# Two tiles of four images become eight units of one image, with the last add of a sampled column on the TensorE

## The chip, the cores and the metric

The kernel runs on one core of a Trainium2 chip, in float32 throughout. The metric is device time in microseconds (us) of one launch. Five engines work side by side, each through its own list of instructions in order, and meet only at semaphores: TensorE (PE; matmuls and transposes, its weight loads are listed as PEld), VectorE (DVE), ScalarE (ACT), GpSimd (POOL), and SyncE (SP, which here only issues transfers).

## The reference

The input is x, 8 images of 32 x 32 pixels with 64 channels. Two layers are added to it one after the other:

```
x = x + L0(groupnorm(x))      # groups of 2 channels, mean and variance over one image
x = x + L1(groupnorm(x))

L0: g, g1 = relu(bn(dwconv3x3(h, wg))), relu(bn(dwconv3x3(h, wg1)))
    gy, gx = sobel(h); Dx = 1/(gy*gy/4 + 1); Dy = 1/(gx*gx/4 + 1)
    D, c0, E, cm_x, cp_x, cm_y, cp_y = ...   # per pixel, from g, g1, Dx, Dy
    for _ in range(5):
        h' = D*(c0*h0 - 2E*h + cm_x*roll(h,1,w) + cp_x*roll(h,-1,w)
                + cm_y*roll(h,1,c) + cp_y*roll(h,-1,c)) + D*0.4*fsrc
        h0, h = h, h'
    return relu(bn(h))

L1: offsets and mask = conv3x3(x, w_offset) + b      # 27 numbers per pixel
    for each of 9 taps: bilinear sample of x at (y + dy, x + dx): 4 corners, 4 weights, times mask
    out = sum over taps and channels of sample * filt
```

L1 needs the finished L0 output of the whole image, since a tap may sample anywhere in it. Images are independent of each other throughout.

## The kernel before

**Tiles.** A tile is 4 images: a partition is an image row (4 x 32 = 128), and the free dimension holds the 32 columns times 64 channels, 2048 numbers. There are two tiles.

**Dense stage of a tile (L0, and the offsets of L1).** Group sums, the squares, the scale; transposes of the normalized input (`turn`), row matmuls for the Sobel gradients (`rows`), the two depthwise convolutions as matmuls with the transposed input as the weights (`conv 0` to `conv 3`), the coefficients, and 5 steps of 4 chunks of 512 numbers (`pde 0` to `pde 19`). In a chunk VectorE makes five products of coefficients and shifted h (L576, L580, L586), TensorE adds them up in a bank of PSUM (L1037), and VectorE adds the rest (L597). A chunk's sums on TensorE run while VectorE makes the next chunk's products, since four chunks are open to it. Then the second norm, the offset convolution, and `sampling`, which turns offsets into table indices and corner weights.

**The table.** The second norm's output is written to a table in HBM (L351): an entry is 1 KB, a pixel with its right, lower and lower right neighbours. At the start the whole table is cleared by 8 transfers (L338), from SP's queue.

**Columns.** A column of a tile is 128 pixels with 9 taps: GpSimd issues 9 indirect transfers (L378), each of which fetches 128 entries. VectorE multiplies the 4 corners of 9 taps by their weights (L748, 2304 numbers; in some columns of tile 0 ScalarE takes three taps, L910), adds lower to upper corners (L755, 1152) and right to left (L761, 576, into `sums`). TensorE transposes the sums, five times 128 x 128 (L1056), ScalarE copies them out of PSUM (L921), and TensorE multiplies by the filter (L1064). Every fourth column VectorE adds a group to x (L730) and SP stores it (L356). There are four pixel buffers. 64 columns x 9 taps are 576 gathers.

**Order.** `SCHEDULE` is a list written by hand: tile 0's dense stage alone, then tile 1's dense stage with tile 0's 32 columns between its pieces, then tile 1's 32 columns alone, in loops. Each engine takes its part of every piece in this order.

## Time and profile before

| | |
|---|---|
| Median of 3 runs | 1076.55 us (1072.9 to 1078.05) |
| Profiled execution, its own time | 1075.92 us |
| its span | 1074.0 us |
| First gather starts, last gather starts | 251.65 us, 1058.04 us |
| PE, DVE, ACT, POOL busy | 57%, 63%, 20%, 59% |
| TensorE clock granted, mean | 0.727 of full |

The page divides the span into 40 slices of 26.85 us. The digits are tenths of busy time, and in the row PEclk tenths of the full clock, 2.4 GHz: a 5 there is the lower of the clock's two levels, 1.2 GHz. A float32 matmul is two instructions; a transpose is one. The duration printed for a matmul contains its way through the array, so the distance between starts is what a row of matmuls costs. "Issue" in front of a gather is time in which GpSimd waits for nothing that the profile shows.

### The profile page before, as it was taken

How to read it: one execution, taken by the hardware profiler on the slowest of the kernel's cores; microseconds unless marked ns; L12 is line 12 of the kernel's file. 1: busy time of each engine (PE TensorE's matmuls, PEld its weight loads, DVE VectorE, ACT ScalarE, POOL GpSimd, SP SyncE). 2: the span in 40 equal slices, each digit the busy share in tenths (PEclk: the TensorE clock that was granted, in tenths of full speed). 3: DMA queues.
4: the chain of work that ended last, by engine and by line, in shares of the span. 5: the costliest groups of instructions: out<-in, count | busy, mean ns of one | idle time of the engine just before them, and what ended most of it. 6: DMA issues, size and time to landing. Idle time of an engine off the chain costs nothing.

```text
span 1074.0 us, 7428 instructions
## 1 busy us (share of the span) xinstructions
PE 612.7 (57%) x2314; PEld 399.3 (37%) x2314; DVE 673.2 (63%) x685; ACT 214.5 (20%) x577; POOL 628.6 (59%) x588
## 2 busy tenths in 40 slices
PE   1987999468985678958843667523222322322233
PEld 1773434123775244434323433323222322322233
DVE  6799999843788676858887446543344334334433
ACT  2721000022523223133213411200000000000000
POOL 0000000004888777877787777777777777777773
PEclk9998999779987878987975686655555555555555
DMA  6431000054222233233222583333333333333331
GB/s 217 132 120 43 0 0 1 0 110 111 84 74 74 79 93 93 77 87 95 85 83 88 133 254 105 93 106 103 107 99 105 107 97 107 101 107 98 106 107 56
DMA packets 58144, 100.35 MB, mean 93 GB/s; under 512 B 10168, under 2 KB 39040, under 8 KB 57856
## 3 DMA queue, kind: packets, MB, share of 16 engines
q0 software_dynamic: 27648, 75.53, 23.8%
q1 hardware_dynamic: 30464, 24.42, 8.4%
q8 instruction: 17, 0.28, 0.1%
q14 instruction: 15, 0.12, 0.0%
HBM read 79.13 MB, written 20.78 MB: 93 GB/s over the span
## 4 chain that ended last, share of the span: by engine, by line
POOL 58%; issue 20%; DVE 12%; PE 5%; ACT 2%; DMA 2%; SPq 1%; POOLq 0%; DVEq 0%
POOL pixels L378 57%; PE acc L1037 3%; DVE rsum L434 2%; SPq L351 1%; DVE shared L586 1%; DVE shared L576 1%; DMA table<-scratch 1%; DVE h_pad L597 1%; DVE shared L556 1%; DVE shared L580 1%; PE acc L959 1%; DMA x<-x_in 0%; DVE scratch L430 0%; DVE scratch L415 0%; PE acc L1005 0%
## 5 line engine op out<-in xcount | busy, mean ns | idle before, releaser
L378 POOL DMA_INDIRECT pixels<-table,index_now x576 | 626.3, 1087 | 180.2 <-issue 172.4
L748 DVE TENSOR_TENSOR pixels<-pixels,side 128x2304 f32<-128x2304 f32 (+1 forms) x64 | 148.2, 2315 | 260.8 <-DMA pixels<-table,index_now 260.4
L1056 PE MATMUL side<-const,sums 128*128 128x128 f32 x320 | 74.1, 388 | 352.7 <-DVE sums L761 324.4
L1037 PE MATMUL acc<-shared,const 128*128 128x512 f32 x400 | 196.1, 635 | 22.7 <-DVE shared L576 22.7
L1056 PEld LDWEIGHTS side<-const,sums 128*128 128x128 f32 x320 | 53.3, 199 | 369.4 <-issue 239.3
L370 POOL COPY index_now<-index 128x72 uint32 x8 | 2.1, 260 | 250.0 <-DMA table<-scratch 250.0
L921 ACT ACTIVATE sampled_T<-side 128x384 f32<-128x384 f32 (+1 forms) x128 | 49.7, 433 | 403.3 <-PE side L1056 403.2
L1064 PEld LDWEIGHTS side<-filt,sampled_T 128*128 128x128 f32 x640 | 126.3, 296 | 0.0
L1064 PE MATMUL side<-filt,sampled_T 128*128 128x64 f32 x640 | 125.8, 373 | 0.0
L1037 PEld LDWEIGHTS acc<-shared,const 128*128 128x128 f32 x400 | 77.8, 202 | 128.0 <-issue 108.3
L755 DVE TENSOR_TENSOR pixels<-pixels 128x1152 f32<-128x1152 f32 x64 | 86.9, 1358 | 7.4 <-ACT pixels L910 5.4
L910 ACT ACTIVATE pixels<-pixels,corner_w 128x64 f32<-128x64 f32 x228 | 56.5, 334 | 135.6 <-DMA pixels<-table,index_now 135.6
L586 DVE TENSOR_TENSOR shared<-arrays,h_pad 128x1024 f32<-128x1024 f32 x40 | 48.8, 1220 | 7.4 <-PE acc L1037 7.3
L580 DVE TENSOR_TENSOR shared<-arrays,h_pad 128x1024 f32<-128x1024 f32 x40 | 48.7, 1219 | 5.5 <-PE acc L1037 5.5
L761 DVE TENSOR_TENSOR sums<-pixels 128x576 f32<-128x576 f32 x64 | 48.5, 758 | 4.9 <-PE side L1056 0.5
L959 PE MATMUL acc<-conv_w,shared 128*128 128x256 f32 x128 | 39.5, 391 | 4.5 <-DVE h_pad L509 4.5
L576 DVE TENSOR_TENSOR shared<-arrays,h_pad 128x512 f32<-128x512 f32 x40 | 27.5, 688 | 18.4 <-ACT h_pad L800 18.4
L935 PE MATMUL acc<-rsum,const 128*128 128x64 f32 x16 | 4.9, 403 | 54.8 <-DVE rsum L434 54.0
L597 DVE TENSOR_TENSOR h_pad<-acc,shared 128x512 f32<-128x512 f32 x40 | 27.4, 685 | 2.1 <-PE acc L1037 2.1
L556 DVE TENSOR_TENSOR shared<-arrays,h_pad 128x512 f32<-128x512 f32 x40 | 27.6, 690 | 0.9
L1035 PE MATMUL acc<-arrays,const 128*128 128x512 f32 x50 | 25.5, 593 | 0.0
L935 PEld LDWEIGHTS acc<-rsum,const 128*128 128x128 f32 x16 | 3.6, 281 | 57.2 <-DVE rsum L434 55.6
(158 smaller groups left out, 744.0 us busy)
## 6 DMA issues: line engine op xcount, KB each, us to landing
table<-corner_w SPq DMA_DIRECT2D x8, 1225.0 KB
pixels<-table,index_now POOLq DMA_INDIRECT x576, 2.8
table<-scratch SPq DMA_DIRECT2D x16, 528.0 KB, 10.4
x<-x_in SPq DMA_DIRECT2D x2, 1024.0 KB, 7.2
out_dram<-x SPq DMA_DIRECT2D x16, 128.0 KB, 1.9
const<-const_in SPq DMA_DIRECT2D x1, 641.0 KB, 6.0
xn_next<-bn_in SPq DMA_DIRECT2D x1, 384.0 KB, 7.1
off_w<-offw_in SPq DMA_DIRECT2D x1, 288.0 KB, 7.1
```

Source lines behind the costliest of these rows:

```text
L378: pool.indirect_dma_start(out=pixels[:, w % COLS, k, :], out_offset=None, in_=table, in_offset=bass.IndirectOffsetOnAxis(ap=index_now[:, o ...
L580: dve.tensor_tensor(two(wc(prod[:, prod_slot(n, 1), :]), wc(prod[:, prod_slot(n, 2), :])), two(coef(2), coef("mid")), two(moved(0, -1), mo ...
L586: dve.tensor_tensor(two(wc(prod[:, prod_slot(n, 3), :]), wc(prod[:, prod_slot(n, 4), :])), two(coef(3), coef(0)), two(moved(-1, 0), moved( ...
L748: dve.tensor_tensor(quads[:, 0:cells, :], quads[:, 0:cells, :], weights[:, 0:cells].unsqueeze(2).to_broadcast([P, cells, C]), ALU.mult)\
L755: dve.tensor_tensor(px[:, :, 0:2 * C], px[:, :, 0:2 * C], px[:, :, 2 * C:4 * C], ALU.add)\
L761: dve.tensor_tensor(sums[:, j % 2, 0:K2 * C].rearrange("p (k c) -> p k c", c=C), px[:, :, 0:C], px[:, :, C:2 * C], ALU.add).then_inc(s_sum ...
L910: ins = act.activation(cell, cell, ACT.Copy, scale=corner_w[:, 0, w, 4 * k + q:4 * k + q + 1])
L921: act.activation(sampled_T[:, j % 2, a * P:b * P], turned[:, r, 0:(b - a) * P], ACT.Copy)\
L959: ins = pe.matmul(dst, turned_pair(dh, pair), w3[:, 0:4 * C], start=dh == 0, stop=False)
L1037: pe.matmul(bank(t, "pde", i), eye, prod[:, prod_slot(n, j), :], start=j == 0, stop=j == PRODS - 1)\
L1056: ins = pe.transpose(turned[:, r, (i - a) * P:(i - a + 1) * P], sums[:, j % 2, i * P:(i + 1) * P], eye)
L1064: ins = pe.matmul(out[:, j * C:(j + 1) * C], sampled_T[:, j % 2, k * P:(k + 1) * P], filt[:, k, :], start=k == 0, stop=k == TAP_PAIRS - 1)
```

## The change

The kernel is written anew around a smaller unit. What it does:

- **Units.** A unit is one image: a partition is an image row of one of four sides (a side is 8 columns wide), and the free dimension holds 8 columns times 64 channels, 512 numbers. There are 8 units. What crosses from a side to its neighbour goes through TensorE, with permuting matrices (`prev`, `next`, `halo`), 20 matrices in the constants instead of 4.
- **Order.** `BESIDE` cuts the dense stage of a unit in 8 parts. Unit 0's runs alone; then part w of unit u+1 stands ahead of column w of unit u, on every engine. In the last unit the columns stand alone.
- **Steps.** A step is one piece of the whole unit. VectorE seeds the target bank in PSUM with c0 times h0 plus the forcing (two instructions of 512), then makes the products from the source bank (two of 1024, one of 512); TensorE adds them shifted into the target (9 matmuls). The next step's products need the finished target.
- **A column** is 128 pixels of one image, again 9 gathers. VectorE multiplies (L529) and adds lower to upper corners (L534); the add of right to left is gone. TensorE transposes left and right parts into the same place, 10 transposes that accumulate in pairs (`flip`), and filters the column before it (`filtered`). There are 7 pixel buffers.
- **Transfers.** Inputs come in 4 transfers for each unit, all queued ahead of the 8 that clear the table. Each unit writes its part of the table with 8 transfers (L304) and needs only its own part before its gathers start. Indices are read in place, no loop is left on any engine.

```diff
-MAKES = {"sum1": [("sum", 0, "dve")], ...
-SCHEDULE = [
-    (0, "sum1, centre1, square1, deviation1, scale1, turn, rows, sobel, denominator, conv 0, gates 0, conv 1, "
...
+BESIDE = ("sum1 centre1 square1 scale1 turn", "grad den conv-0 log seed", "dterms conv-1 da own coef",
+          "pde-0 pde-1", "pde-2 pde-3", "pde-4 final sum2 centre2", "square2 scale2 halo turn2", "off samp")
+ORDER = [(0, piece) for part in BESIDE for piece in part.split()]
+for u in range(UNITS):
+    for w in range(WS):
+        if u + 1 < UNITS:
+            ORDER += [(u + 1, piece) for piece in BESIDE[w].split()]
+        ORDER.append((u, f"column-{w}"))
...
+            load_x(0)
...
+            for u in range(1, UNITS):
+                load_x(u)
             sp.wait_ge(s_zeros, 1)
             for b in range(B):
                 sp.dma_start(table[b * TY * TX:(b + 1) * TY * TX, :] ...).then_inc(s_cleared, 16)
             sp.wait_ge(s_cleared, 16 * B)
...
+            for u in range(UNITS):
+                pool.wait_ge(s_table, 16 * TABLE_DMAS * (u + 1))
+                pool.wait_ge(s_index, u + 1)
+                for w in range(WS):
+                    col = u * WS + w
+                    if col >= NB:
+                        pool.wait_ge(s_weighted, col - NB + 1)
+                    for k in range(K2):
+                        pool.indirect_dma_start(out=pixels[:, col % NB, k, :], ...)
...
+            def step(u, m):          # VectorE
+                seq(dve.tensor_tensor(target(m), c0[:, :], source(m) if m == 0 else target(m), ALU.mult))
+                dve.tensor_tensor(target(m), target(m), force[:, :], ALU.add).then_inc(s_seeded, 1)
+                if m:
+                    dve.wait_ge(s_h, n)
+                for dirs in (slice(1, 5, 2), slice(2, 5, 2)):
+                    dve.tensor_tensor(prod[:, dirs, :], coef[:, dirs, :],
+                                      source(m).unsqueeze(1).to_broadcast([P, 2, WC]), ALU.mult).then_inc(s_prod, 1)
+                dve.tensor_tensor(prod[:, 0, :], coef[:, 0, :], source(m), ALU.mult).then_inc(s_prod, 1)
...
-                dve.tensor_tensor(sums[:, j % 2, 0:K2 * C].rearrange("p (k c) -> p k c", c=C),
-                                  px[:, :, 0:C], px[:, :, C:2 * C], ALU.add).then_inc(s_sums, 1)
+                upper, lower = weighted[:, col % 2, 0:2, 0:K2, :], weighted[:, col % 2, 2:4, 0:K2, :]
+                dve.tensor_tensor(upper, upper, lower, ALU.add).then_inc(s_added, 1)
...
+            def column(col):         # TensorE
+                pe.wait_ge(s_added, col + 1)
+                for r, (a, b) in enumerate(PARTS):
+                    for k in range(a, b):
+                        for q in range(2):
+                            ins = flip(turned[:, r, (k - a) * P:(k - a + 1) * P],
+                                       weighted[:, col % 2, q, 2 * k:2 * k + 2, :].rearrange("p k c -> p (k c)"),
+                                       eye, q == 0, q == 1)
+                    ins.then_inc(s_part, 1)
+                if col:
+                    filtered(col - 1)
```

How the order of instructions moves is shown at three places. First TensorE in the kernel before, at a column of tile 0 between the convolutions of tile 1: L959 to L964 are the convolutions, L1056 the transposes of a column, L1064 its filter.

```order
L959 MATMUL acc<-conv_w,shared 128x256
L961 MATMUL acc<-conv_w,shared 128x128
L964 MATMUL acc<-conv_w,shared 128x128
L1056 MATMUL side<-const,sums 128x128 x5
L1064 MATMUL side<-filt,sampled_T 128x64 x5
L959 MATMUL acc<-conv_w,shared 128x256
```

The same place in the changed kernel, column 1 of a unit between the two convolution banks of the next: `conv_w,xT` are the convolutions, `const,weighted` the transposes.

```order
L697 MATMUL banks<-conv_w,xT 128x128
L700 MATMUL banks<-const,weighted 128x128 x10
L697 MATMUL banks<-filt,sampled_T 128x64 x5
L697 MATMUL banks<-bn_shift,const 128x512
L697 MATMUL banks<-conv_w,xT 128x128
L697 MATMUL banks<-conv_w,xT 128x384 x2
```

A column's transposes are ten instead of five, and the second half of a unit's convolution stands behind them in TensorE's list.

VectorE in the kernel before, a column inside the steps of tile 1: L576 to L586 are products of a chunk, L597 its end, L748 to L761 the column, L556 the next chunk's start.

```order
L580 TENSOR_TENSOR shared<-arrays,h_pad 128x1024
L586 TENSOR_TENSOR shared<-arrays,h_pad 128x1024
L597 TENSOR_TENSOR h_pad<-acc,shared 128x8x64
L740 COPY side<-corner_w 128x144
L748 TENSOR_TENSOR pixels<-pixels,side 128x1536
L755 TENSOR_TENSOR pixels<-pixels 128x9x128
L761 TENSOR_TENSOR sums<-pixels 128x576
L556 TENSOR_TENSOR shared<-arrays,h_pad 128x512
```

VectorE in the changed kernel, the end of `pde-1`, column 3, and the start of `pde-2`: L455 and L456 seed, L463 and L465 are products, L529 and L534 the column.

```order
L463 TENSOR_TENSOR prod<-coef,banks 128x2x512 x2
L465 TENSOR_TENSOR prod<-coef,banks 128x512
L529 TENSOR_TENSOR weighted<-pixels,banks 128x9x4x64
L534 TENSOR_TENSOR weighted<-weighted 128x2x576
L455 TENSOR_TENSOR banks<-c,banks 128x512
L456 TENSOR_TENSOR banks<-banks,force 128x512
L463 TENSOR_TENSOR prod<-coef,banks 128x2x512 x2
```

A column is two instructions instead of three, and stands after every second whole step instead of between chunks.

SP in the changed kernel, from the last small input to the first table write: 28 transfers of units 1 to 7 stand ahead of the 8 that clear the table; before, one transfer (x of tile 1) stood there.

```order
L283 DMA filt<-filt_in 128x320
L265 DMA x_1<-x_in 32x512 x4
L265 DMA x_2<-x_in 32x512 x4
L265 DMA x_3<-x_in 32x512 x4
L265 DMA x_4<-x_in 32x512 x4
L265 DMA x_5<-x_in 32x512 x4
L265 DMA x_6<-x_in 32x512 x4
L265 DMA x_7<-x_in 32x512 x4
L289 DMA table<-corner_w 1225x1x256 x8
L304 DMA table<-xn 32x9x128 x2
L304 DMA table<-xn 32x8x128 x6
```

The clearing has moved behind 28 transfers, and the first table write behind it is a quarter of a tile's.

## Rows read from the trace of the kernel before

**Rows 1.** The page: span, busy time, slices of POOL and clock, chain.

```profile
span 1074.0 us, 7428 instructions
PE 612.7 (57%) x2314; PEld 399.3 (37%) x2314; DVE 673.2 (63%) x685; ACT 214.5 (20%) x577; POOL 628.6 (59%) x588
POOL 0000000004888777877787777777777777777773
PEclk9998999779987878987975686655555555555555
POOL 58%; issue 20%; DVE 12%; PE 5%; ACT 2%; DMA 2%; SPq 1%; POOLq 0%; DVEq 0%
```

**Rows 2.** Windows: PE, PEld, DVE, ACT, POOL busy, clock, DMA share, GB/s.

```profile
250.00:664.00 414.00, 293.37 (x1116) 180.86 (x1115) 297.16 (x312) 125.15 (x382) 327.54 (x278) 0.81 0.35 99
664.00:1058.00 394.00, 124.08 (x545) 110.18 (x543) 165.68 (x135) 31.32 (x84) 299.91 (x305) 0.52 0.35 103
```

**Rows 3.** Groups by form: busy us, mean ns | idle before, releasers.

```profile
L378 POOL DMA_INDIRECT pixels<-table,index_now x576 | 626.3, 1087 | 180.2 <-issue 172.4 <-POOL index_now L370 7.1 <-DVE sums L761 0.6
L748 DVE TENSOR_TENSOR pixels<-pixels,side 128x2304 f32<-128x2304 f32 x45 | 114.9, 2554 | 244.7 <-DMA pixels<-table,index_now 244.5
L755 DVE TENSOR_TENSOR pixels<-pixels 128x1152 f32<-128x1152 f32 x64 | 86.9, 1358 | 7.4 <-ACT pixels L910 5.4
L580 DVE TENSOR_TENSOR shared<-arrays,h_pad 128x1024 f32<-128x1024 f32 x40 | 48.7, 1219 | 5.5 <-PE acc L1037 5.5
L761 DVE TENSOR_TENSOR sums<-pixels 128x576 f32<-128x576 f32 x64 | 48.5, 758 | 4.9 <-PE side L1056 0.5
L597 DVE TENSOR_TENSOR h_pad<-acc,shared 128x512 f32<-128x512 f32 x40 | 27.4, 685 | 2.1 <-PE acc L1037 2.1
L861 ACT ACTIVATE arrays<-acc 128x512 f32<-128x512 f32 x16 | 9.0, 632 | 1.7 <-PE acc L1005 1.6
L873 ACT ACT_TABLE_LOAD x2 | 2.6, 1283 | 0.0
L640 DVE TENSOR_TENSOR arrays<-arrays 128x144 f32<-128x144 f32 x2 | 0.6, 308 | 0.1
```

**Rows 4.** Timeline of TensorE at full clock: start, duration, instruction.

```profile
9.21 0.69 PE L935 MATMUL acc<-rsum,const 128*128 128x64 f32 x2 [9.21 <-DVE rsum L434]
...
115.13 0.19 PEld L1037 LDWEIGHTS acc<-shared,const 128*128 128x128 f32 x1 [0.24 <-issue]
...
464.48 0.53 PEld L1056 LDWEIGHTS side<-const,sums 128*128 128x128 f32 x5 [1.86 <-DVE sums L761]
...
464.98 1.20 PEld L1064 LDWEIGHTS side<-filt,sampled_T 128*128 128x128 f32 x10
```

**Rows 5.** Timeline near the end, clock at its lower level.

```profile
1042.38 0.93 PEld L1056 LDWEIGHTS side<-const,sums 128*128 128x128 f32 x5 [8.37 <-DVE sums L761]
...
1058.04 0.94 POOL L378 DMA_INDIRECT pixels<-table,index_now  x1 [0.30 <-issue]
```

**Rows 6.** Windows around an idle stretch of TensorE (columns as rows 2).

```profile
340.00:345.00 5.00, 0.55 (x4) 0.36 (x3) 4.74 (x4) 3.38 (x6) 4.05 (x4) 0.50 0.36 105
345.00:350.00 5.00, 5.00 (x18) 3.97 (x19) 4.93 (x4) 0.00 (x0) 4.43 (x2) 0.50 0.17 52
350.00:355.00 5.00, 5.00 (x11) 2.15 (x10) 4.93 (x3) 0.00 (x0) 4.39 (x3) 0.84 0.18 52
```

**Rows 7.** Table transfers by line: ns min/median/max, first and last start.

```profile
L351 SPq DMA_DIRECT2D table<-scratch x16: 302/2692/3941, 224.5 to 624.8; - x16
L338 SPq DMA_DIRECT2D table<-corner_w x8: 957/10293/11264, 4.9 to 68.2; - x8
```

**Rows 8.** Window in which the clearing ends (columns as rows 2).

```profile
90.00:95.00 5.00, 5.00 (x13) 2.23 (x12) 4.96 (x3) 0.00 (x0) 0.00 (x0) 1.00 0.05 16
```

**Rows 9.** Timeline: a VectorE instruction with two SBUF inputs, and a gather.

```profile
319.38 2.29 DVE L492 SCALAR_TENSOR_TENSOR arrays<-arrays 128x2048 f32<-128x2048 f32 x1
...
320.46 2.02 POOL L378 DMA_INDIRECT pixels<-table,index_now  x1 [0.30 <-issue]
```

More of the change, by code:

```diff
@@ L23 @@
 STEPS = 5
+NDIR = 5
 LO = 2
@@ L57 @@
-C_ENT = C_BASE + W * 2 * K2
-C_ALL = C_ENT + TILES
-MAKES = {"sum1": [("sum", 0, "dve")], "square1": [("sum", 1, "dve")], "sum2": [("sum", 2, "dve")],
-         "square2": [("sum", 3, "dve")], "turn": [("turn", q, "act") for q in range(NBANK)],
-         "rows": [("rows", q, "act") for q in range(2 * NBANK)],
-         "own sums": [("own", q, "dve") for q in range(NBANK)],
-         "turn2": [("turn2", q, "act") for q in range(NBANK)]}
-MAKES.update({f"conv {i}": [("conv", q, "dve") for q in (2 * i, 2 * i + 1)] for i in range(4)})
@@ L118 @@
-COLUMN = ("weigh column", "turn column", "copy column")
-ORDER = [(0 if "column" in part or part.startswith("scale ") else tile, part)
-         for tile, pieces in SCHEDULE for piece in pieces.split(", ")
-         for part in (COLUMN if piece == "column" else (piece,))]
-PLAN = [(t,) + made for t, piece in ORDER for made in MAKES.get(piece, [])]
-AT = {made[:3]: n for n, made in enumerate(PLAN)}
+PARTS = ((0, 4), (4, TAP_PAIRS))
+NB = 7
+TABLE_DMAS = 2 * SIDES
+NAMES = ("ones", "eye", "prev", "next", "diff", "diff2", "smooth", "smooth_neg",
+         "diff_in_left", "diff_at_left", "diff_in_right", "diff_at_right",
+         "smooth_neg_in_left", "smooth_neg_at_left", "smooth_in_right", "smooth_at_right",
+         "minus", "prev_neg", "next_neg", "halo")
@@ L194, in build_program @@
[L194 to L203 removed]
+        x1 = [sb(f"x1_{u}", [P, WC]) for u in range(UNITS)]
@@ L780, in _ @@
+            for u, part in ORDER:
+                name, _, i = part.partition("-")
+                piece(u, name, int(i or 0))
+            add_group(UNITS * GROUPS_U - 1)
         @block.scalar
@@ new lines, in norm_root, with turned_main @@
+            def norm_root(u, which):
+                act.wait_ge(*emptied(u, f"square{which}"))
+                act.activation(grstd[:, :], gvar[:, :], ACT.Sqrt, bias=gn_eps).then_inc(s_sd, 1)
+            def turned_main(u, what):
+                act.wait_ge(s_full, full(u, what, 0))
+                for dh in (1, 0, 2):
+                    ins = act.activation(*shifted_rows(rows(xT[:, dh, 0:PAIRS * P]), rows(bank(u, what, 0)), dh),
+                                         ACT.Copy)
+                ins.then_inc(s_act, 1)
@@ L927, in _ @@
+            act.wait_ge(s_setup, 1)
+            prepare(ACT.Sqrt)
+            for u, part in ORDER:
+                name, _, i = part.partition("-")
+                piece(u, name, int(i or 0))
         @block.tensor
         def _(pe):
-            def group_sums(t, k):
-                pe.wait_ge(s_rsum, 2 * norm_index(t, k // 2 + 1) + k % 2 + 1)
-                if t == 0 and k == 0:
-                    pe.wait_ge(s_const, 16)
-                wait_bank_empty(pe, t, "sum", k)
-                pe.matmul(bank(t, "sum", k)[:, 0:C], ones_block, rsum[:, :], start=True, stop=True).then_inc(s_bank, 1)
@@ L1049, in turn_part, with wait_bank_empty @@
[L1049 to L1060 removed]
+            def wait_bank_empty(u, what, q=0):
+                n = AT[u, what, q]
+                before = [f for f in PLAN[:n] if f[3] == PLAN[n][3]]
+                if before and before[-1][4]:
+                    pe.wait_ge(*emptied(*before[-1][:3]))
```

1378 lines of the change are left out of this document (617 added, 761 removed).

## The prediction

> **What bounds the kernel now.** I read the page first: its slices show GpSimd empty for the first nine, then at 7 to 8 tenths to the end, and its chain puts 58% on GpSimd and 20% on "issue", which is the time between gathers [rows 1]. So the kernel is 251.65 us of work ahead of the first gather, then 576 gathers in a row, then a tail. The windows give the pace: 305 gathers in the last 394 us, 1.29 us each, 11.6 us for a column of 9 [rows 2]. The last gather starts at 1058.04, so the tail behind it is 1074.0 - 1058.04 = 16.0 us [rows 1, 5]. While the first tile's gathers ran beside the second's dense stage they came at 1.49 us each (414 / 278) [rows 2]. VectorE is 63% busy and TensorE 57%, and neither sets the end [rows 1]: the dense work of tile 1 is hidden behind tile 0's gathers, because big instructions of a four-image tile keep several banks open, and a wait of one finds work in another.
>
> The profiled execution took 1075.92 us, 1.9 more than its span and within 0.1% of the median; the sums below are made against it.
>
> **What the change does to this.** The gathers stay 576, of the same shape. What is bought is the head: the first gather needs one image, not four. What is paid is that seven dense stages, each of one image, now stand in the same in-order lists as the columns, and that within a unit nearly every piece waits for the one before. So the question is the period S of a unit: what is longer, 8 columns of gathers (93 us), or the chain of a dense stage with 8 columns in it.
>
> **Prices.** TensorE at full clock: weight loads of a row of 512-column matmuls start 0.19 + 0.24 = 0.43 us apart, so a float32 matmul (two instructions) of 512 columns costs 0.86, of 448 0.75, of 384 0.64, and of 128 or fewer 0.22, since ten weight loads take 1.20 and five transposes 0.53 [rows 4]. Behind the last one the result takes about 0.45 more: two 64-column instructions take 0.69 in all [rows 4]. VectorE: 512 numbers 0.69, 1024 1.22, and a column 2.55 + 1.36 = 3.9 without the add of 0.76 that goes; small ones 0.2 to 0.3 [rows 3]. ScalarE: 0.63 for 512, a table load 1.28 [rows 3]. TensorE's share of a column is 10 transposes and 10 filter instructions, 1.1 + 1.2 = 2.3.
>
> **The period, part by part**, at full clock, each from VectorE's end of one column to its end of the next. TensorE starts each part with the 2.3 of the column just ended.
> - Part 0: 2.3, group sum 0.9 + 0.45, reduce and centre 1.0, square 0.6, sum 1.35, reduce, root, reciprocal and three small ones 1.8, scale 0.7, six transposes 1.1, copies 0.9, weights 0.3, column 3.9 = 15.4.
> - Part 1: 2.3, gradients 5.6 (two of 448 and four of 64 make 2.4, one of 512, two of 448 and four of 64 make 3.2), then conv-0 with 0.86 + 3 x (0.22 + 0.64 + 0.64 + 0.22) = 6.0. ScalarE's logarithm stands in its list behind conv-0's relu, so it comes at 2.3 + 5.6 + 6.0 + 0.4 + 0.6 = 14.9, takes 0.7, the exponential 1.28 + 0.6, then five VectorE instructions 3.6, column 3.9 = 25.2. TensorE is idle for 11 us of it: the other half of the convolution stands behind this column's transposes.
> - Part 2: 2.3, conv-1 6.0, latency and relu 1.1, then TensorE's own sums 4.1 + 0.4 beside VectorE's gate and coefficient work, the last coefficient 0.7, column 3.9 = 18.6.
> - Parts 3 and 4, two steps each: seeds 1.4 and first product 1.2, TensorE's nine matmuls 1.9 + 2.1 + 0.9 = 4.9 + 0.4, products 3.0, column 3.9 = 14.9 each, 0.3 more for one copy of weights. TensorE's second step (1.2 + 4.9) ends as the column does, so nothing is gained by the column in its shadow.
> - Part 5: one step 7.9, the shift and add 2.8, sum, mean and centre 2.4, column 3.9 = 17.0.
> - Part 6: 2.3, sum 1.4, root chain 1.7, scale 0.7, transposes 1.3, copies 0.9, column 3.9 = 12.2.
> - Part 7: 2.3, offsets (19 matmuls, all small) 4.3 + 0.4, sampling 8 instructions to the index 2.5, 7 more 2.2, column 3.9 = 15.7.
>
> The sum is 134.2 us. It is longer than the 93 us of gathers, so GpSimd will wait for indices, which come only in part 7, and S is this chain.
>
> **The clock.** TensorE has 75 us of work in these 134, with idle stretches of 4 to 11 us. In the trace of before such a stretch costs the clock: TensorE was idle from 340 to 345, granted 0.50, and was busy all of 345 to 350 at 0.50 still; the higher level came back in the next window (0.84) [rows 6]. That is some 6.6 us of work at half speed, and at half speed five transposes take 0.93 instead of 0.53 [rows 4, 5]. Parts 1 and 2 begin behind such a stretch: 3.3 us lost each. Part 3 loses 2.5, part 0 runs at the low level whole (column +1.8, two sums and transposes +2.9: 4.7), part 6 loses 3.9, part 7 4.5. Together 22 us, so S = 156.
>
> The Trainium skill says in "TensorE: Matmul & The Clock Gate", "What's actually happening", that the throttled clock is the default and activity releases it. By that rule the low level in parts with gaps is what to expect, and rows 6 agree (0.50 behind the idle stretch); with the clock always released the sum would be that of the rival below.
>
> **The sum.** Clearing the table bounds the first gather. It was issued from 4.9 on and its transfers were nearly over in the window from 90 to 95 (DMA share 0.05), some 87 us [rows 7, 8]. Now 28 loads at about 0.4 us of issue and some small ones stand ahead: from 17.5 to 105. Unit 0's dense stage alone is the chain without columns, 134 - 8 x (3.9 + 2.3) = 85 us, so it is hidden by the clearing. The table write adds its issue (8 transfers of about 280 pieces against 1056 for 2.7 us: 0.7 each) and 5 to land: first gather at 116. Its bounds: 90 (the dense stage alone) and 130.
> - First column of unit 0: 9 gathers and landing 13, column 4: to 133.
> - Parts 1 to 7 of unit 1: 156 - 20 = 136: to 269.
> - Six more units: 6 x 156 = 936: to 1205.
> - Unit 7 has no unit beside it. Its index came 6 us before: 71 distances of 1.29 = 91.5, and the tail 16.0 (0.76 less on VectorE, 0.9 more for the transposes): 1205 - 6 + 0.5 + 91.5 + 16 = 1307, and with the 1.9 outside the span **1309 us**, 22% slower.
>
> A microsecond of S counts seven times. S would have to be 122 us to reach 1076.
>
> **Unknown prices.** Transposes that accumulate do not occur in the trace: between nothing more than now (0.107 each) and as a full matmul of 128 columns (0.22), which gives 1.1 for a column and 8 x 7 x 1.1 = 60 us in all; I take the lower, as the same instruction. Reads of shifted or broadcast operands on TensorE: no change against up to 10% of 60 us a unit, 40 us in all, I take none. Hand-overs between engines are in the prices above where rows have them; some 60 in a period at 0 to 0.1 us more are 0 to 6 us of S. Gathers may be faster or slower beside this VectorE work; GpSimd has 60 us of slack in a period, so this is nothing.
>
> **Rivals.**
> - The clock stays high. TensorE is at work in every part, and the window 250 to 664 had a mean of 0.81 with 71% busy [rows 2]. Then S = 134 and the time is 1309 - 7 x 22 = 1155. Against it: the idle stretches above are as long as that in rows 6. The chance is 0.17.
> - More waits than I see, or the dear end of the transposes: S of 170 and more, 1405 and up. 0.15.
> - Gathers set the pace (the other sign). If the dense chain hid in the gathers as tile 1's does now, S would be 8 x 11.6 plus, between units, what the index comes late: column 6 3.9, TensorE's part and offsets 7.0, sampling 2.5, start 0.5 = 14 and landing 2.8, less the 11.6 of column 7's gathers: 5. S = 98, and the time 1309 - 7 x 58 = 903. For it: VectorE's own work is only some 90 us a unit. Against it: in-order lists, and three hand-overs in each step. It decides where S falls below 122, 12 us under my sum at full clock. 0.05.
> - The change as a trade of VectorE for TensorE: a column saves 0.76 on VectorE and pays 0.5 to 0.9 on TensorE in the same chain; alone it would be worth under 0.3 us a column, 15 us in all, and decides nothing.
>
> In that third rival the pace of gathers would matter. A gather beside a VectorE instruction with both inputs in SBUF took 2.02 us, against 0.94 alone, ending with it [rows 5, 9]. The Trainium skill, "SBUF — State Buffer", "SBUF: two separate sides", has such an instruction hold the port that GpSimd shares. Now most have one operand in PSUM; by that rule the pace is nearer 1.25 than 1.49, and the sum stays as it is.
>
> **How the numbers follow.** Forecast: S about 156, own range 1210 to 1400, chance 0.63. Clock high 0.17 (1155, down to 1110), more waits 0.15, faster or no change 0.05. The 8-in-10 range is 1140 to 1410. Within 0.5% is about what runs of this kernel can't tell from none. Faster by more 0.04, within 0.01, slower 0.95.
>
> **What would show it.** First gather near 116; gathers in eight bursts of some 95 us with idle stretches of some 60 between, ended by VectorE's index; 156 us from unit to unit; part 1 the longest with TensorE idle in it; a granted clock near 0.75; VectorE and TensorE both under 65% busy and waiting for each other in the steps. I am wrong if gathers are even to the end, if the first starts after 130, or if a part takes 5 us less than its sum.

## The result and the profile after

The changed kernel takes 1275.89 us (median of 4 runs, 1272.1 to 1277.78); the kernel before took 1076.88 in the same runs. The ratio is 1.185, 95% interval 1.181 to 1.189: slower by 18.5%. The forecast was 1309. The profiled execution took 1272.1 us, 2.2 more than its span. Runs over 1.5% above the fastest of their kernel are in a slower state and enter no comparison; below, that holds for two runs of one kernel. First the page: span, busy time, slices of TensorE, GpSimd and the granted clock, and the chain by engine and by line (31.7 us a slice).

```profile
span 1269.9 us, 9355 instructions
PE 801.5 (63%) x3472; PEld 598.6 (47%) x3472; DVE 616.9 (49%) x836; ACT 205.5 (16%) x403; POOL 564.8 (44%) x589
PE   6764578546875668656585558855677565865434
POOL 1002774067710776027740477107760177503773
PEclk9885789557896679857787678965798568875555
PE 44%; DVE 30%; SPq 7%; issue 7%; POOL 6%; DMA 3%; ACT 3%; POOLq 0%; DVEq 0%
```

Before, GpSimd's row had nine empty slices and then none [rows 1]; now it has eight bursts with a gap behind seven of them, and the chain that was 58% GpSimd is 74% TensorE and VectorE. The 195.9 us between the two spans add up so: the first gather comes 135.1 earlier (116.58 against 251.65); the gathers themselves take 64.7 less (561.6 against 626.3, [rows 3]); GpSimd idles 403 us between gathers beyond the usual 0.30, against 8.5 before; the end behind the last gather is 1.0 longer. The groups, as in [rows 3] (busy, mean ns of one | idle before, releasers):

```profile
L343 POOL DMA_INDIRECT pixels<-table,index x576 | 561.6, 975 | 688.5 <-issue 575.4 <-DMA table<-xn 112.9 <-DVE weighted L529 0.3
L529 DVE TENSOR_TENSOR weighted<-pixels,banks 128x2304 f32<-128x2304 f32 x64 | 163.2, 2550 | 70.0 <-DMA pixels<-table,index 54.2 <-issue 14.9
L700 PE MATMUL banks<-const,weighted 128*128 128x128 f32 x640 | 137.4, 392 | 342.4 <-DVE weighted L534 342.4
L463 DVE TENSOR_TENSOR prod<-coef,banks 128x1024 f32<-128x1024 f32 x80 | 93.9, 1215 | 61.4 <-PE banks L697 61.4
L534 DVE TENSOR_TENSOR weighted<-weighted 128x1152 f32<-128x1152 f32 x64 | 86.9, 1358 | 2.2
```

TensorE stood idle for 342 us in front of the transposes of columns, waiting for VectorE's L534. One period of the middle, cut where VectorE ends a column: parts 0 to 7 of a unit (length; busy PE, PEld, DVE, ACT, POOL; clock, DMA share, GB/s).

```profile
715.76:733.76 18.00, 8.49 (x42) 7.61 (x42) 8.26 (x16) 4.75 (x9) 13.74 (x15) 0.59 0.36 106
733.76:760.36 26.60, 15.65 (x73) 11.43 (x73) 8.25 (x10) 7.19 (x11) 20.20 (x22) 0.82 0.34 102
760.36:780.46 20.10, 15.18 (x67) 11.14 (x68) 9.61 (x15) 3.78 (x9) 15.23 (x17) 0.84 0.38 111
780.46:798.56 18.10, 16.38 (x58) 10.51 (x59) 12.37 (x13) 0.77 (x2) 13.84 (x15) 0.79 0.38 109
798.56:813.53 14.97, 12.73 (x58) 7.66 (x58) 12.62 (x14) 0.77 (x2) 2.47 (x3) 1.00 0.09 27
813.53:830.10 16.57, 9.85 (x49) 6.22 (x49) 10.36 (x12) 1.40 (x3) 0.00 (x0) 0.97 0.00 0
830.10:845.76 15.66, 8.21 (x37) 7.52 (x38) 6.89 (x13) 4.35 (x9) 0.00 (x0) 0.50 0.36 72
845.76:866.95 21.19, 12.77 (x80) 12.67 (x80) 7.80 (x17) 3.25 (x7) 7.53 (x8) 0.67 0.17 46
```

No engine is full in any of them; nearest are TensorE in part 3 (90%) and TensorE and VectorE in part 4 (85 and 84%). GpSimd is done with a unit in part 4 and stands idle until part 7 gives it the next index. Now inside part 1, the longest, in the timeline (start, duration, instruction, idle before):

```profile
733.89 2.40 PE L700 MATMUL banks<-const,weighted 128*128 128x128 f32 x10 [5.17 <-DVE weighted L534]
737.55 5.82 PE L697 MATMUL banks<-xn,const 128*128 128x448 f32 x26
744.11 5.37 PE L697 MATMUL banks<-conv_w,xT 128*128 128x128 f32 x24
749.52 0.60 ACT L657 ACTIVATE gates<-banks 128x512 f32<-128x512 f32 x1 [5.54 <-PE banks L697]
750.01 0.71 ACT L661 ACTIVATE log_t<-t_arr,scalars 128x512 f32<-128x512 f32 x1
750.74 1.28 ACT L663 ACT_TABLE_LOAD   x1
752.67 0.69 DVE L417 SCALAR_TENSOR_TENSOR t_arr<-t_arr,banks 128x512 f32<-128x512 f32 x1 [7.97 <-ACT banks L663]
756.31 2.55 DVE L529 TENSOR_TENSOR weighted<-pixels,banks 128x2304 f32<-128x2304 f32 x1
760.31 1.97 PE L700 MATMUL banks<-const,weighted 128*128 128x128 f32 x8 [10.82 <-DVE weighted L534]
```

Gradients, the first half of the convolution, relu, logarithm, table load, VectorE's five, the column: one behind the other, with TensorE idle for 10.8 us at the end of it.

### The profile page after: what moved, and what is told of

Same layout as the page of the kernel before. It is cut to its first block, busy times and chain, and to the rows that moved or that the text cites. A ratio compares the mean times of both kernels' runs of the same rounds, so it can differ in the third digit from the quotient of the medians.

```text
span 1269.9 us, 9355 instructions
## 1 busy us (share of the span) xinstructions
PE 801.5 (63%) x3472; PEld 598.6 (47%) x3472; DVE 616.9 (49%) x836; ACT 205.5 (16%) x403; POOL 564.8 (44%) x589
## 4 chain that ended last, share of the span: by engine, by line
PE 44%; DVE 30%; SPq 7%; issue 7%; POOL 6%; DMA 3%; ACT 3%; POOLq 0%; DVEq 0%
PE banks L697 35%; DVE weighted L529 11%; PE banks L700 9%; POOL pixels L343 6%; DVE weighted L534 6%; SPq L289 5%; DVE prod L463 3%; DMA table<-corner_w 2%; SPq L265 1%; DVE banks L456 1%; DVE xn L378 1%; ACT L663 1%; DVE banks L455 1%; ACT gates L657 1%; DVE prod L465 1%
## 5 line engine op out<-in xcount | busy, mean ns | idle before, releaser
L343 POOL DMA_INDIRECT pixels<-table,index x576 | 561.6, 975 | 688.5 <-issue 575.4
L700 PE MATMUL banks<-const,weighted 128*128 128x128 f32 x640 | 137.4, 392 | 342.4 <-DVE weighted L534 342.4
L700 PEld LDWEIGHTS banks<-const,weighted 128*128 128x128 f32 x640 | 114.1, 205 | 365.4 <-DVE weighted L534 350.6
L697 PE MATMUL banks<-prod,const 128*128 128x448 f32 (+2 forms) x720 | 219.2, 457 | 31.4 <-DVE prod L463 31.4
L529 DVE TENSOR_TENSOR weighted<-pixels,banks 128x2304 f32<-128x2304 f32 x64 | 163.2, 2550 | 70.0 <-DMA pixels<-table,index 54.2
L697 PEld LDWEIGHTS banks<-prod,const 128*128 128x128 f32 x720 | 114.8, 201 | 120.2 <-issue 120.2
L697 PEld LDWEIGHTS banks<-filt,sampled_T 128*128 128x128 f32 x640 | 124.7, 293 | 0.0
L463 DVE TENSOR_TENSOR prod<-coef,banks 128x1024 f32<-128x1024 f32 x80 | 93.9, 1215 | 61.4 <-PE banks L697 61.4
L697 PE MATMUL banks<-filt,sampled_T 128*128 128x64 f32 x640 | 123.0, 368 | 0.0
L697 PE MATMUL banks<-conv_w,xT 128*128 128x384 f32 (+1 forms) x384 | 89.5, 391 | 0.0
L534 DVE TENSOR_TENSOR weighted<-weighted 128x1152 f32<-128x1152 f32 x64 | 86.9, 1358 | 2.2
```

The lines of the kernel that those rows point to most:

```text
L343: pool.indirect_dma_start(out=pixels[:, col % NB, k, :], out_offset=None, in_=table, in_offset=bass.IndirectOffsetOnAxis(ap=index[:, at:at ...
L463: dve.tensor_tensor(prod[:, dirs, :], coef[:, dirs, :], source(m).unsqueeze(1).to_broadcast([P, 2, WC]), ALU.mult).then_inc(s_prod, 1)
L529: dve.tensor_tensor(weighted[:, col % 2, :, 0:K2, :].rearrange("p q k c -> p k q c"), pixels[:, col % NB, :, :].rearrange("p k (q c) -> p ...
L534: dve.tensor_tensor(upper, upper, lower, ALU.add).then_inc(s_added, 1)
L697: return pe.matmul(dst, lhsT, rhs, start=start, stop=stop, skip_group_check=True)
L700: return pe.matmul(dst, data, moved, start=start, stop=stop, is_transpose=True, skip_group_check=True)
```

## The experiments

The theory: the chain of one unit's dense stage with eight whole columns in it sets the period (150.2 us from index to index in the middle six units), and the low clock of TensorE behind its idle stretches is part of it. The rivals: gathers set it; or the trade of a VectorE add for transposes matters more than the forecast said.

**Conv-1 ahead of column 1.**

```diff
-"grad den conv-0 log seed", "dterms conv-1 da own coef"
+"grad den conv-0 log seed conv-1", "dterms da own coef"
```

> The second half of a unit's convolution (conv-1) stands right behind the first in every list, ahead of column 1 instead of behind it; nothing else moves. Chain theory: TensorE works in the stretch of 10.8 us in which it now waits for column 1, and part 2 (20 to 22.5 us now) loses the 6.0 us of the convolution; its remaining sums (4.1 us at full clock, 8.2 at the lower) still start after column 1's transposes, so part 2 becomes 14 to 17 us. The period falls from 150.2 to about 145, the time from 1276 to about 1235 (1225 to 1245). Rival, that the period is set by the amount of work on VectorE or by gathers: the same work in another order, so no change (1270 to 1282).

Measured: 1221.99 us (1220.08 to 1222.77), ratio 1.136 to before (1.134 to 1.138); period 143.4. It is 54 us less than the changed kernel: part 2 fell from 20.9 (mean) to 14.4, and one piece moved ahead of one column, in the lists of TensorE and ScalarE, did it; the other parts moved by -1.5 to +2.1 and nearly cancel. The theory held, with a little more gained than its range (1225 to 1245) allowed.

**Columns where VectorE waits, inside the parts.** `|` marks the column.

```diff
+"sum1 centre1 | square1 scale1 turn", "grad den conv-0 | log seed", "dterms conv-1 | da own coef",
+"pde-0 | pde-1", "pde-2 | pde-3", "pde-4 | final sum2 centre2", "| square2 scale2 halo turn2", "off | samp"
```

> The same instructions, but each column stands inside its part, where VectorE waits for another engine, and not behind it: behind centre1, behind conv-0, behind conv-1, between two steps, behind the single step, ahead of square2, behind off. Chain theory: a column's 3.9 us on VectorE lies in a wait: 2.4 us less in part 0, 3.9 in part 1, some 9 in part 2 (the column, and conv-1 which now starts behind conv-0), 1.4 in parts 3 and 4 each (two steps are 13 us in any case), 3.9 in part 5, 2.5 in part 6, 3.9 in part 7, together about 28. Period 122, time about 1080 (1060 to 1130). Rival, amount of work: no change. Rival, that gathers set it: no change either, since they are the same.

Measured: 1179.89 us (1179.3 to 1180.24), ratio 1.097 (1.095 to 1.099); period 136.5, not 122. Missed by 100 us. The timeline shows one reason: column 0 now stands ahead of its pixels, whose gathers begin only behind the index.

```profile
659.34 0.20 DVE L501 TENSOR_SCALAR index<-above 128x72 uint32<-128x72 f32 x1
...
662.93 0.63 ACT L646 ACTIVATE squares<-xc 128x512 f32<-128x512 f32 x1 [1.47 <-DVE xc L370]
673.02 2.56 DVE L534 TENSOR_TENSOR weighted<-pixels,banks 128x2304 f32<-128x2304 f32 x1 [9.90 <-issue]
...
677.02 2.39 PE L705 MATMUL banks<-const,weighted 128*128 128x128 f32 x10 [15.37 <-DVE weighted L539]
679.21 1.74 PE L702 MATMUL banks<-filt,sampled_T 128*128 128x64 f32 x10
680.79 1.11 PE L702 MATMUL banks<-squares,const 128*128 128x128 f32 x8
```

And the marker moved TensorE's part of a column together with VectorE's: the sum of squares, ready at 663.6, stands behind both at 680.8. A column has to be cut into its parts, each placed for its own engine.

**The third add back on VectorE.**

```diff
+                dve.tensor_tensor(left, left, right, ALU.add).then_inc(s_added, 1)
...
-                        for q in range(2): ins = flip(..., weighted[:, col % 2, q, ...], eye, q == 0, q == 1)
+                        ins = flip(..., weighted[:, col % 2, 0, ...], eye)
```

> The part of the change that its name speaks of, undone alone: VectorE adds right to left corners as well (576 numbers, 0.76 us), TensorE transposes 5 times in a column instead of 10. Chain theory: 0.76 us more in each of the 8 columns of a period and 0.5 (full clock) to 1.1 us (lower clock) less on TensorE in the same chain: between -0.3 and +0.3 us a column, so 1276 within 10 us either way. Rival, that accumulating transposes are dear: faster by 30 us or more. Rival, that VectorE's amount of work sets the pace: 7 x 8 x 0.76 = 43 us slower.

Measured: 1317.73 us (1315.37 to 1320.59), ratio 1.225 (1.222 to 1.228); period 157.2, clock 0.71. So that part of the change, alone, is worth 42 us, nearly three times the 15 that the prediction had as its bound. The rival "amount of work on VectorE" had 43 and met the number, but not as a mechanism: VectorE is 49% busy in the changed kernel, and with the same work in the woven order below a period is 47 us shorter. Two more runs below go into it.

**TensorE kept busy** with useless matmuls while it waits for a column.

```diff
+FILL = (16, 40, 12, 0, 0, 16, 16, 30)
+                if 0 < col < (UNITS - 1) * WS:
+                    pe.wait_ge(s_sT, (col - 1) * len(PARTS) + 1)
+                    for i in range(FILL[col % WS]): mm(turned[:, 0, 0:P], eye, M["ones"], True, True)
```

> TensorE gets matmuls whose result nobody uses (16, 40, 12, 0, 0, 16, 16, 30 of 128 columns ahead of columns 0 to 7), in the stretches in which it waits for a column's add, into a place that the transposes behind them overwrite. They should end before the add does at full clock. Clock theory: the granted clock rises from 0.74 to over 0.9, the period falls by 10 to 14 of the 16 us by which it exceeds the 134 of full clock: 1165 to 1205 us. Rival, that the lower clock lies where nothing waits for TensorE: clock up, time unchanged or a little more, since the extra matmuls can only be in the way (1270 to 1300).

Measured: 1174.24 us (1173.8 to 1175.8), ratio 1.0925 (1.090 to 1.095); clock 0.884, period 136.5. The time was inside the forecast, the clock stayed just under the 0.9 forecast. Adding work took 102 us off: the low clock is 13.7 us of a period at least. Three parts of it, 0, 3 and 6 (columns as above):

```profile
797.05:812.62 15.57, 11.13 (x73) 10.75 (x74) 8.30 (x15) 4.75 (x9) 11.91 (x13) 0.78 0.37 108
722.55:737.19 14.64, 12.75 (x56) 7.67 (x56) 12.33 (x14) 0.77 (x2) 11.29 (x12) 1.00 0.36 107
768.73:781.48 12.75, 10.06 (x64) 9.87 (x65) 7.13 (x14) 4.34 (x9) 0.00 (x0) 0.73 0.42 84
```

They last 18.0, 18.1 and 15.7 in the changed kernel at 0.59, 0.79 and 0.50. The forecast's sums at full clock were 15.4, 14.9 and 12.2. Part 2 gained nothing: it took 21.5 at 0.84 with the fillers and 20.9 at 0.80 to 0.84 without, against a sum of 18.6 at full clock.

**The third add at a high clock**: the last two edits together.

> The third VectorE add back (five plain transposes a column), with the useless matmuls that held the clock at 0.884 and 1174 us. Without them the third add cost 42 us (1318 against 1276) at a lower clock (0.71 against 0.743). Theory A 'the trade is near even, the 42 us came by the clock': at a high clock +0.76 on VectorE and -0.53 on TensorE, 0.23 x 56 = 13 us, 1187. Theory B 'VectorE's add stands in the chain whole, TensorE's transposes of the column before mostly don't': +0.76 x 56 = 43 us, 1217.

Measured: 1229.76 us at a clock of 0.847 and 1248.14 at 0.839, ratio 1.152 (1.142 to 1.162). The other two runs took 1255.01 (the profiled one, 0.825) and 1257.87 (0.829) and are not compared. The size is rough, then: 56 to 74 us over the run with fillers alone. Both theories missed, on the same side. What is firm is parts that ran at clock 1.00 with the add and without it. Part 1, this run (25.2 in each of its six middle units, 25.0 with the fillers alone), and part 4, from the run with the third add and no fillers (14.97 in the changed kernel):

```profile
723.59:748.81 25.22, 22.54 (x147) 18.33 (x147) 8.82 (x10) 7.19 (x11) 19.13 (x21) 1.00 0.36 105
```

```profile
833.60:849.38 15.78, 12.20 (x51) 7.12 (x51) 13.40 (x15) 0.77 (x2) 0.02 (x1) 1.00 0.03 9
```

Where TensorE's column leads the part, the trade costs 0.2, as the forecast had it. In the steps VectorE's seeds cover TensorE's transposes, so the five that are saved give nothing back and the add counts whole, 0.8. As an estimate from these two parts, with three columns in the steps and five elsewhere, that makes 3 x 0.8 + 5 x 0.2 = 3.4 us a period, 24 in all. The rest of the 42 I put down to the clock (0.743 to 0.71); this pair of runs doesn't show it alone, but the later run with this edit in another order does for its own case.

**A third of the gathers.** Only taps 0 to 2 are fetched (`for k in range(3)`, `pixels[:, :, 3:K2, :]` zeroed once).

> Only taps 0 to 2 of each column are fetched (192 gathers instead of 576), the other six are zeros written once at the start; VectorE and TensorE do all they did. Leaves out the samples of six taps. Theory 'the chain of dense stage and columns sets the period': the index period stays at 148 to 152 us, since nothing in it waits for a gather but column 0 after the index (54.2 us of waits for pixels in all, x7, 7.7 each). Of these 7.7 some 7.5 go (6 gathers less), so the period falls to about 143; the last unit's columns, 11.5 apart now, come at VectorE's and TensorE's own pace of 6 to 7 (-36 us), and the first column comes 7.5 earlier. Sum 1276 - 7 x 7.5 - 36 - 7.5 = 1180, 1160 to 1230. Theory 'gathers set the pace': a column costs 9 x 1.25 = 11.3 in every unit, and 3.8 with a third of them: 64 x 7.5 = 480 us less, about 800.

Measured: 1210.37 us (1198.96 to 1213.15), ratio 1.1235 (1.117 to 1.131); the last six periods have a mean of 150.4. With 384 gathers less the period did not move: gathers don't set it, and the rival is out. The time lies in the expected range (1160 to 1230), but the period of 143 was missed: I had put the 54.2 us of waits for pixels into the period. 9.2 of them stand in front of the first column of all and the other 45 in the last unit, whose columns now come 4.1 apart instead of 11.6 (7 x 7.5 = 52 of the 66 us gained). GpSimd's row and its idle time:

```profile
POOL 4000600033000430003300043000430004300043
L344 POOL DMA_INDIRECT pixels<-table,index x192 | 188.1, 979 | 988.5 <-DVE index L497 828.4
```

**The woven order.** Each column is cut: V is VectorE's part, T that of TensorE and ScalarE. Columns begin in unit 1's stage behind `den`, and those left at the end follow unit 7's. ScalarE takes the logarithm ahead of the first convolution's relu and loads the table of Exp there; the inputs of units 2 to 7 are queued behind the clearing.

```diff
+WOVEN = ("sum1 centre1 V square1 T scale1 turn grad den V log conv-0 T seed conv-1 dterms V da own "
+         "coef T pde-0 pde-1 V T pde-2 pde-3 V T pde-4 V final sum2 T centre2 V square2 T scale2 "
+         "halo turn2 off V samp T")
...
                     seq(act.activation(log_t[:, :], t_arr[:, :], ACT.Ln, bias=log_const))
+                    prepare(ACT.Exp)
```

> The dense stage of a unit keeps its pieces and their order, but each column is cut in VectorE's part and TensorE's with ScalarE's part, and each is put where its engine waits for the dense stage: VectorE's behind a sum or a product that TensorE still has to turn into something, TensorE's behind what VectorE still has to answer; the logarithm stands ahead of the first convolution's relu; the loads of units 2 to 7 are queued behind the clearing. Theory 'the chain sets the period, and the columns cost because they stand in it': of 8 x (3.9 + 2.3) = 50 us a period most falls into waits, so the period is 107 to 120 and the time 1276 - 7 x (150 - 113) - 10 = 1007, 970 to 1080. Rival 'engines are full': VectorE's own work of 617 / 8 = 77 us and TensorE's of 100 us a unit at this clock leave no room, the columns push the dense work back wherever they stand, as in the order with whole columns inside the parts (period 136.5): 1150 to 1200.

Measured: **937.65 us** (933.86 to 943.04), ratio 0.871 (0.868 to 0.873) to the kernel before: it beats both kernels, by 12.9% and by 26.5%. The theory had its sign right and its size too small (period 107 to 120, 970 to 1080 us); the rival "engines are full" (1150 to 1200) is out. The page, one whole period, and a column in the steps:

```profile
PE 721.9 (77%) x3472; PEld 533.9 (57%) x3472; DVE 613.3 (65%) x836; ACT 204.9 (22%) x411; POOL 588.6 (63%) x589
POOL 1000177766777577757777677747776777757772
PEclk9988597987999699979998799968999899955555
L362 POOL DMA_INDIRECT pixels<-table,index x576 | 585.4, 1016 | 335.9 <-issue 219.6
```

```profile
442.30:546.50 104.20, 86.70 (x436) 63.77 (x435) 75.59 (x103) 25.35 (x51) 75.04 (x74) 0.92 0.37 106
```

```profile
470.46 2.55 DVE L548 TENSOR_TENSOR weighted<-pixels,banks 128x2304 f32<-128x2304 f32 x1
473.05 1.36 DVE L553 TENSOR_TENSOR weighted<-weighted 128x1152 f32<-128x1152 f32 x1
474.46 1.31 PE L723 MATMUL banks<-const,weighted 128*128 128x128 f32 x10 [0.31 <-DVE weighted L553]
475.61 1.23 PE L720 MATMUL banks<-filt,sampled_T 128*128 128x64 f32 x10
477.01 5.18 PE L720 MATMUL banks<-prod,const 128*128 128x448 f32 x18 [0.18 <-DVE prod L482]
```

The same 836 VectorE instructions and 3472 of TensorE as in the changed kernel, with eight table loads more on ScalarE, take 103.1 us a period instead of 150.2 (last six of each); from the first index to the last it is 724.2 instead of 1053.8, 329.5 of the 338 us gained. The column lies in the shadow of TensorE's sums, TensorE waits 0.31 and 0.18 us in it, and the clock of this period is 0.92 with no filler. The loads moved behind the clearing brought only 2.4 us: the first gather starts at 114.2, since unit 0's index comes at 107.7 either way (107.1 in the changed kernel).

**The woven order with 30 useless matmuls a unit** (`F-6`, `F-8`, `F-6`, `F-10`).

> As the woven order, with 30 useless 128 x 128 matmuls a unit on TensorE at four places where it still waits for VectorE, only to hold the clock. Theory 'what is left is the low clock': granted clock over 0.85, the period 98 to 107, 930 to 985 us, faster than the kernel before (1075). Rival 'the woven order has no gaps to fill': the 30 matmuls (6.6 us at full clock) add to the period what they last, +5 us a period, 35 us more than the woven order alone.

Measured: 955.74 us (954.26 to 958.4), ratio 0.889 (0.887 to 0.891), clock 0.878, period 105.8. The theory's range (930 to 985) holds this, but it held no change as well; its claim that the low clock is what is left failed, since the clock rose and the time too. The rival had the sign and twice the size: where there are few gaps, fillers cost 18 us, not 35.

**The woven order with the third add back** (the edit as above).

> The woven order with the third VectorE add of a column (576 numbers, 0.76) and five plain transposes instead of ten that accumulate. In the order with whole columns this cost 42 us (1318 against 1276). Theory 'an instruction costs what of it stands in the chain': the columns of the woven order end mostly inside waits, so only the 3 among the steps and the one in each norm pay 0.76 each, 7 x 3 = 21 us at most, and TensorE gives 0.55 back in some: 940 to 960. Rival 'VectorE's add counts whole wherever it stands': 56 x 0.76 = 43, 980 and more.

Measured: 1006.37 us (1006.12 to 1008.15), ratio 0.9365 (0.934 to 0.939), clock 0.778 against 0.861, period 112.7. It costs 69 us: the theory (21 at most) missed, and the rival's 43, with its top left open, is too little. The column in the steps again, and the step behind it, which has no column:

```profile
503.91 0.76 DVE L557 TENSOR_TENSOR weighted<-weighted 128x576 f32<-128x576 f32 x1
504.72 0.77 PE L727 MATMUL banks<-const,weighted 128*128 128x128 f32 x5 [1.10 <-DVE weighted L557]
505.32 1.23 PE L724 MATMUL banks<-filt,sampled_T 128*128 128x64 f32 x10
507.27 6.75 PE L724 MATMUL banks<-prod,const 128*128 128x448 f32 x18 [0.72 <-DVE prod L483]
515.43 5.18 PE L724 MATMUL banks<-prod,const 128*128 128x448 f32 x18 [1.41 <-DVE prod L483]
```

TensorE waits 1.10 and 0.72 instead of 0.31 and 0.18, has five transposes less, and its 18 instructions take 6.75 instead of 5.18, at a granted clock of 0.76 instead of 1.00. So it is behind each of the three columns in the steps, in every middle period (6.7 to 6.8). The length of one wait doesn't tell it: the next step's sums, behind a wait of 1.41, took 5.18 at 1.00. Three times 1.6 by the clock and 0.8 by the add are 7 of the 9.6 us that a period is longer. The third add takes its own time and, with TensorE idle for longer on both sides of a column, part of its neighbour's.

**Two columns at the denominator, two in the steps** (`grad V den log V conv-0 T seed conv-1 T dterms V da own coef T pde-0 pde-1 pde-2 V T pde-3 pde-4 V ...`, the columns one later).

> The woven order (937.7 us, period 102.8 from index to index) with one of its three columns among the five steps moved to where VectorE waited 5.8 us for the gradients, so that two columns stand ahead of and behind the denominator there, and three instead of two transposed columns between the two convolutions and behind them. Columns of a unit run one later. Theory 'the period is the chain, and a column in the steps costs it what it is longer than TensorE's sums' (8.4 us for a step with a column, 6.6 for one without): -1.8 us, and -1.9 where TensorE's part stands closer behind; period 99 to 101, 915 to 930 us. Rival 'GpSimd is the bound now' (72 x 1.33 = 96, 6.7 us idle in a period): no room below 96 but this one is the same as far as it goes. Rival 'TensorE between the convolutions is the bound': one more column of 2.3 there, period 105, 950 us.

Measured: 947.32 us (941.96 to 947.81), ratio 0.880 (0.876 to 0.883), period 103.7. No gain, 10 us more: the theory missed, and the rival "TensorE between the convolutions" (105, 950) is nearest.

**No column in the first norm** (the same front part, three columns in the steps).

> As the run with two columns at the denominator, but all three columns stay among the steps and none stands in the first norm, where TensorE's part delayed the transposes by 1.9 us (at the lower clock) and VectorE's the reduction by 1.9. Theory chain: 3.8 less in the norm, against the woven order: period 99, 915 us. Rival 'the clock': with nothing for TensorE in the norm, it is granted 0.50 in the gradients behind it (+3 to 5 us), period 102 to 104, 935 to 950 us.

Measured: 955.93 us (953.7 to 959.6), ratio 0.889 (0.886 to 0.893), period 105.9. The theory (99, 915) missed. The rival "the clock" had the sign, and more came than it said (102 to 104, 935 to 950). The window of off, samp and the next unit's norm up to its gradients:

```profile
732.87:754.96 22.09, 17.65 (x78) 15.29 (x79) 11.67 (x29) 6.78 (x13) 10.98 (x12) 0.60 0.29 78
```

In the woven order the same stretch, from 7.0 us ahead of an index to 15.1 behind it, was granted 0.66 to 0.85 in the middle units.

**The logarithm behind the relu again** (`grad den V conv-0 log T`, no early table load).

> The woven order with the logarithm put back behind the first convolution's relu in ScalarE's list, and the table of Exp loaded behind it, not ahead. Theory 'ScalarE's list is in the chain': logarithm 0.7 and table load 1.28 come behind the relu, so VectorE's five instructions start 2.7 us later, of which 1 to 2.7 reach the end: period +1 to +2.7, 945 to 957 us. Rival 'the second convolution on TensorE ends later anyway' (it ends 0.4 us ahead of the column that stands behind the five instructions): 938 to 942.

Measured: 957.04 us (956.23 to 959.49), ratio 0.8905 (0.888 to 0.893), period 105.9. It came out at the theory's upper edge (945 to 957) and far from the rival (938 to 942): ScalarE's list is in the chain. The 19 us aren't its price alone, though, as the end of the next section says.

## Why the prediction was right, and where not

- **What binds.** Right. The dense chain sets the period: with a third of the gathers it stayed; with the same instructions in another order it fell by a third.
- **The head.** Forecast 116, measured 116.58. The last transfer of the clearing was issued at 82.9, and SP went on 26.3 later, at 109.2, with the table write. Two errors met here: the end of the clearing was forecast at 105, and the write and its landing at 11 instead of the 7.3 that they took, so the 116 is in part luck. And unit 0's dense stage, 85 us in the forecast and so "hidden by the clearing", was off: its index came at 107.1. So the lower bound of 90 wasn't there to be had, as the woven run shows (114.2).
- **First column and unit 1.** Forecast 133 and 269; measured 133.4 and 265.9.
- **The period.** Forecast 156, measured 150.2. By parts 0 to 7 (forecast with the clock, then measured mean): 20.1 and 18.5, 28.5 and 27.5, 21.9 and 20.9, 17.4 and 17.4, 15.2 and 15.0, 17.0 and 16.6, 16.1 and 15.3, 20.2 and 19.1. The order of the parts was right, none is off by more than 1.6. The term mis-sized is the clock: 22 us a period forecast, 13.7 measured between this kernel and the one with TensorE kept busy (whose parts 0, 2 and 6 still show 0.78, 0.84 and 0.73, so more than 13.7, and how much more isn't shown). In part an error of the other sign hid it: that kernel has 136.5 where the forecast had 134.2 at full clock, with part 2 alone 2.9 over its sum. (The terms printed for parts 0 to 3 and 7 add up to 0.1 to 0.2 less than their sums, 0.6 in all, which changes nothing.) The error is (156 - 150.2) x 6 = 35 and the 3 of unit 1: the span was forecast at 1307 and is 1269.9.
- **The end.** Index of unit 7 to the end of column 7 before it: 6 forecast, 6.2 measured. From column 7's end to the end of the span 102 forecast, 102.9 measured.
- **Clock high, 1155.** The price was right (1174 with TensorE kept busy), the condition did not come by itself.
- **Gathers set the pace, 98 us and 903.** It did not come with this order. The woven order comes near its numbers (103.1 and 937.7) and provides its condition, the columns hidden in waits, but not its mechanism: a period holds 72 x 1.32 = 95 us of gathers and GpSimd still idles 7.5, and between the first unit and the last VectorE never waits for pixels. What ends GpSimd's wait is the index, so the dense chain is still what is seen to bind; whether fewer gathers would help there wasn't tried.
- **Transposes that accumulate.** The low bound was right: 10 take 1.26 to 1.31 at full clock, 0.11 apart, as five plain ones take 0.77.
- **The trade alone, "under 15 us".** Wrong: 42 us in this order, 69 in the woven one. The step that failed is "a column saves 0.76 on VectorE and pays 0.5 to 0.9 on TensorE in the same chain". In the steps they are not in the same chain (0.8 against 0), and a VectorE instruction ahead of a waiting TensorE also costs clock. The forecast of the whole didn't suffer, since its parts were summed with the column as the changed kernel has it, without the add.
- **The pace of gathers.** 0.975 + 0.30 = 1.275 us with the dense work beside them (1.27 to 1.29 in each unit), nearer 1.25 than 1.49, as expected of instructions with an operand in PSUM. The Trainium skill, "SBUF — State Buffer", "SBUF: two separate sides", agrees with this and with [rows 9]. The prediction read there that the gather ended with VectorE's instruction; it ended 0.8 us behind it (322.48 against 321.67).

Left open: the 330 us of the woven order were not split further than the logarithm (19), the loads (2) and, in the whole-column order, conv-1 (54). Three woven orders (fillers, no column in the norm, the logarithm behind) settle at periods of 105.8 to 105.9, and the woven order itself has single periods of 106; two other edits, columns inside the parts and TensorE kept busy, share 136.5. What draws them to one value wasn't found. The time isn't lost in one place: with the logarithm behind, the first step's sums take 7.1 us in the later periods instead of 5.18, with the fillers 5.18, and both periods are 105.8. So differences of 2 to 3 us a period between woven orders, and the 19, 10 and 18 us that follow from them, have a share that isn't the price of their edit.

## What to carry to other kernels

Before a tile is made smaller to start a pipeline earlier, add up the chain of one small tile with what is put between its pieces: here it saved 135 us of head and paid some 57 us over the gathers' own time in each of seven periods, and the sum of the parts, from rows of the old trace, came within 4% of it. When two jobs share in-order engines, place each engine's part of the second job on its own, in a wait that this engine has, and look where its input will be by then. The price of an instruction is not its duration: ahead of a waiting TensorE it can also cost clock, and with wide gaps even useless matmuls pay (102 us), while with narrow ones they don't.

## What the runs showed of the hardware

- In the changed kernel, 130 useless matmuls of 128 columns a unit in the waits raised the granted clock from 0.743 to 0.884 and took 8% off the time (1275.9 to 1174.2); 30 a unit in an order without such gaps raised it from 0.861 to 0.878 and added 2%.
- In the woven order with the third add TensorE was idle for 1.10 us in front of a column in the steps and 0.72 behind it, without it 0.31 and 0.18, and the 18 instructions that follow took 6.75 us at a granted 0.76 instead of 5.18 at 1.00. A wait of 1.41 in front of a step without a column left the clock at 1.00. The Trainium skill, "TensorE: Matmul & The Clock Gate", "What's actually happening", has the throttled clock as the default, which activity releases; the runs agree as far as more idle time goes with less clock.
- Indirect gathers were 1.28 us apart on the mean in the changed kernel and 1.32 in the woven order. In the woven order all 85 gathers that ran inside VectorE's L548 (one operand in PSUM) kept their 0.94 to 0.95; the 64 that began inside the column's second instruction, L553, whose operands are all in SBUF, took 1.58 on the mean and up to 2.13. In the timeline of the woven kernel:

```profile
493.92 0.94 POOL L362 DMA_INDIRECT pixels<-table,index  x1 [0.30 <-issue]
496.07 1.36 DVE L553 TENSOR_TENSOR weighted<-weighted 128x1152 f32<-128x1152 f32 x1
496.41 1.84 POOL L362 DMA_INDIRECT pixels<-table,index  x1 [0.30 <-issue]
```
